# Rounding the keys to their high half on GpSimd instead of ScalarE, from the second batch on

## The chip, the cores and the metric

One core of one Trainium2 chip runs the whole program. The metric is the device time of one execution in microseconds (us). The kernel before takes 885.71 us, the median of 3 runs. PE is TensorE's matmul side and PEld its weight loads, DVE is VectorE, ACT is ScalarE, POOL is GpSimd, SP is SyncE, which here only issues DMA transfers.

## The reference

One block of a small network, in float32, on 8 batches of 512 tokens of width 256: cross-attention with 16 heads of width 16 in which the context serves as keys and as values, and then a mixture of 8 experts, of which each token uses its two best.

```python
x = x + xattn(layernorm(x), ctx, ctx, w_proj, b_proj)   # x, ctx: (8, 512, 256)
x = x + ffn(layernorm(x), Wg, W1, W2, W3)

# xattn: q = x / 2, k = cond_k / 2, 16 heads of width 16
scores = einsum('bthd,bshd->bhts', q, k)
w = softmax(scores, axis=-1)
out = einsum('bhts,bshd->bthd', w, v) @ w_proj.T + b_proj

# ffn: the top 2 of 8 experts, hidden width 682
gating = softmax(where(in_top_2, x @ Wg.T, -inf))
expert_out = (silu(x @ W1[e].T) * (x @ W2[e].T)) @ W3[e].T
out = sum over e of gating[e] * expert_out[e]
```

## The kernel before

**Precision.** A float32 operand of a matmul is split into a float16 high half and a float16 low half (the rest that the rounding leaves), and the products of the halves are summed. For the keys of batch b, `kt_in` (128 x 2 x 512, float32, 512 KB) is the loaded block, `k16[0]` its rounding to float16 and `k16[1]` the low half `kt_in - k16[0]`. There is one `kt_in`, one `k16[0]` and one `k16[1]`, used by all batches in turn. `k_stack` (two, batch b uses `b % 2`) holds for each pair of heads three bands of rows: high, low and high halves of the keys. Six DMA transfers of 128 KB each (two for each band) copy them there from `k16`: `k_part`, line 490. Queries go the same way through `x_in`, `q16`, a transpose on PE, `qt16` and `q_stack`.

**Order of the work.** There is no scheduler at run time. Each engine runs its own list of instructions strictly in order and waits on semaphores. The lists are written by one loop over slots, `for slot in range(FIRST, LAST)`, the same for every engine. A batch advances every 16 slots. A piece of work with offset `AT_...` stands in slot `16 * b + AT_...` of its engine's list. A slot is a place in a list, not a time: an engine can be ahead of another.

In each slot of the attention PE makes the scores of two units in both orientations. DVE takes the maximum of one (line 970), ACT the exponential of the other (line 839), and PE weighs the values with the exponentials (line 1294). Three pairs of PSUM banks go round between them, so that PE can be only a little ahead of DVE and ACT.

**The path of the keys.** For batch b from 1 on:
- SP, slot 16b-22: waits for `s_kl >= b` (the low half of batch b-1 is made) and loads `kt_in` of batch b (line 595). Right behind it in the same slot are the six `k_part` transfers of batch b-1, which wait for the same semaphore (line 598) and read `k16`; each adds 16 to `s_kd`.
- ACT, slot 16b-18 (`AT_K_HI`, lines 908 to 911): waits for the load (`s_kin`) and for `s_kd >= 96 b`, which says that all six transfers of batch b-1 have landed, so that `k16` is free, and rounds `kt_in` to `k16[0]`.
- POOL, slot 16b-4 (`AT_K_LO`): `low_keys`, line 691, makes `k16[1]`.

**POOL's list in the slots around.** By slot modulo 16, for the batches that are in flight at once:
- 12: `low_keys` (691), then `choose` (697 to 715), which waits for DVE's indices of the two best experts
- 14: `split_weights(e, 2)` (746 to 756), which prepares a third of an expert's weights
- 1: `pick_slots` (720 to 728)
- 2: `inverse_root` for the layer norm in front of the attention (678 to 686, `AT_X_ROOT`), `finish_rows` (733, 737) and `scatter` (eight indirect transfers, 472)
- 3: `split_weights(e, 0)`
- 4: `inverse_root` for the second layer norm (`AT_Z_ROOT`)
- 5: the low half of the queries (794, `AT_Q_LO`)
- 7: `split_weights(e, 1)`
- 8: the low half of the tokens for the experts and a copy (802, 806, `AT_Z_LO`)

`choose`, `pick_slots` and `scatter` belong to a batch whose attention is done, so they first run in the slots 44 to 50, beside the keys of batch 4. The work on ACT that needs POOL's results is `normalise` (844): on the queries in the slots 0 to 2 modulo 16 (needs `AT_X_ROOT`) and on the tokens in slot 5 (needs `AT_Z_ROOT`). ACT rounds the normalised tokens in slot 8 (928), for which POOL's line 802 waits. PE needs POOL's low half of the queries at line 1328.

After the last batch the experts run tile by tile on PE; the first tiles are interleaved with the end of the attention.

Of the kernel before, what the change touches and what calls it, by code (L numbers as in the profile page):

```python
# [99 lines left out]
AT_K_HI = -18  # L100
# [43 lines left out]
def piece_at(half_slot):  # L144
    return 0 <= half_slot - EARLY_HALF < EARLY * PIECES


def due(step, offset, of=1):

    b, left = divmod(step - offset, PER * of)  # L150
    return [b] if left == 0 and 0 <= b < B else []
# [36 lines left out]
def hold(eng, passed):  # L188

    eng.sem_inc(passed, 1)  # L190
# [53 lines left out]
def ge(eng, sem, value):  # L244
    if value > 0:
        eng.wait_ge(sem, value)
# [22 lines left out]
def build(nc, xq_l, x_l, v_l, kT_l, wp_l, bias, wg_l, w12_l, w3_l, const, out):  # L269
    ctx = ExitStack()  # L270
    with ctx:
# [3 lines left out]
        def sem(name):  # L275
            return ctx.enter_context(nc.semaphore(name))
# [84 lines left out]
        def se(name, shape, dt=F32):  # L361
            return spent.enter_context(nc.sbuf_tensor(name, shape, dt))

        x_in = se("x_in", [P, NT, W])
        kt_in = se("kt_in", [P, 2, T])
        q16 = [se(f"q16_{i}", [P, NT, W], F16) for i in range(2)]
        qt16 = [se(f"qt16_{i}", [P, 2, T], F16) for i in range(2)]
        k16 = [se(f"k16_{i}", [P, 2, T], F16) for i in range(2)]
# [38 lines left out]
        s_xin, s_kin, s_vin, s_xres_ld = sem("s_xin"), sem("s_kin"), sem("s_vin"), sem("s_xres_ld")  # L407
        s_qh, s_kh = sem("s_qh"), sem("s_kh")
        s_ql, s_kl = sem("s_ql"), sem("s_kl")
        s_qd, s_kd = sem("s_qd"), sem("s_kd")  # L410
# [258 lines left out]
        def _(pool):  # L669
# [6 lines left out]
            def inverse_root(agg, rs, sh, done, b):  # L676

                nc.gpsimd.tensor_tensor(rs[:, :], agg[:, :, 1], con[:, C_EPS:C_EPS + 1].to_broadcast([P, NT]),
                                        ALU.add).then_inc(done, 1)
                pool.wait_ge(done, b * 4 + 1)  # L680
                nc.gpsimd.tensor_tensor(rs[:, :], rs[:, :], con[:, C_POW:C_POW + 1].to_broadcast([P, NT]),
                                        ALU.pow).then_inc(done, 1)
                pool.wait_ge(done, b * 4 + 2)
                nc.gpsimd.tensor_tensor(sh[:, :], agg[:, :, 0], rs[:, :], ALU.mult).then_inc(done, 1)
                pool.wait_ge(done, b * 4 + 3)
                nc.gpsimd.tensor_tensor(sh[:, :], sh[:, :], con[:, C_NEG:C_NEG + 1].to_broadcast([P, NT]),
                                        ALU.mult).then_inc(done, 1)

            def low_keys(b):
                pool.wait_ge(s_kh, b + 1)  # L690
                nc.gpsimd.tensor_tensor(k16[1][:, :, :], kt_in[:, :, :], k16[0][:, :, :],
                                        ALU.subtract).then_inc(s_kl, 1)
# [24 lines left out]
            def pick_slots(b):  # L717

                pool.wait_ge(s_diff, b + 1)
                nc.gpsimd.tensor_tensor(ediff[:, :], con[:, C_EULER:C_EULER + 1].to_broadcast([P, NT]), diff[:, :],  # L720
                                        ALU.pow).then_inc(s_ed, 1)
                pool.wait_ge(s_ed, b + 1)
                nc.gpsimd.tensor_scalar(den[:, :], ediff[:, :], 1.0, WSCALE, ALU.add, ALU.mult).then_inc(s_den, 1)
                pool.wait_ge(s_pos, b + 1)
                if b >= 1:
                    pool.wait_ge(s_slot, b * 3)
                for c in range(2):
                    nc.gpsimd.tensor_tensor(pick[:, c, :, :], hot[:, c, :, :], pos[:, :, :],
                                            ALU.mult).then_inc(s_pick, 1)

            def finish_rows(b):

                nc.gpsimd.tensor_copy(z_row[:, :, :, W].bitcast(U32),
                                      con[:, C_TOK + b * NT:C_TOK + (b + 1) * NT].unsqueeze(1).broadcast_to([P, 2, NT])
                                      ).then_inc(s_row, 1)
                pool.wait_ge(s_gate, b + 1)
                nc.gpsimd.tensor_tensor(z_row[:, 1, :, W + 1], ediff[:, :], z_row[:, 0, :, W + 1],
                                        ALU.mult).then_inc(s_row, 1)
# [41 lines left out]
                            add_rows(k, k % 2, t, k)  # L780

            for slot in range(FIRST, LAST):
                for b in due(slot, AT_K_LO):
                    if b >= 1:
                        low_keys(b)
                for b in due(slot, AT_X_ROOT):
                    pool.wait_ge(s_prep, (b + 1) * K_STAT)
                    ge(pool, s_qn, b * NT)
                    inverse_root(mv, rstd, shift, s_rstd, b)
                    if b == 0:  # L790
                        low_keys(b)
                for b in due(slot, AT_Q_LO):
                    pool.wait_ge(s_qh, b + 1)
                    nc.gpsimd.tensor_tensor(q16[1][:, :, :], x_in[:, :, :], q16[0][:, :, :],
                                            ALU.subtract).then_inc(s_ql, 1)
                for b in due(slot, AT_Z_ROOT):
                    pool.wait_ge(s_ln2, (b + 1) * K_STAT)
                    ge(pool, s_zn, b * NT)
                    inverse_root(mv2, rstd2, shift2, s_rstd2, b)
                for b in due(slot, AT_Z_LO):  # L800
                    pool.wait_ge(s_zh, b + 1)
                    nc.gpsimd.tensor_tensor(z_row[:, 0, :, W // 2:W].bitcast(F16), z_n[:, :, :],
                                            z_row[:, 0, :, 0:W // 2].bitcast(F16), ALU.subtract).then_inc(s_zl, 1)
                    pool.wait_ge(s_zl, b + 1)
                    hold(pool, s_held[2])
                    nc.gpsimd.tensor_copy(z_row[:, 1, :, 0:W], z_row[:, 0, :, 0:W]).then_inc(s_zcp, 1)
                for b in due(slot, AT_CHOOSE):
                    choose(b)
                for b in due(slot, AT_PICK):
                    pick_slots(b)  # L810
                for b in due(slot, AT_SCATTER):
                    finish_rows(b)
                    scatter(pool, b)
                for c, off in enumerate(AT_W_LO):
                    for e in due(slot, off):
                        split_weights(e, c)
                for h in range(2):
                    add_early(2 * slot + h)
# [9 lines left out]
        def _(act):  # L828
# [65 lines left out]
            for slot in range(FIRST, LAST):  # L894
                exponentials(slot, 0)
                misc(2 * slot)
                if piece_at(2 * slot):
                    next(early)
                exponentials(slot, 1)
                for b, s in running(slot, AT_WEIGH):  # L900
                    if s % 4 == 3:
                        g = s // 4
                        q = b * 4 + g
                        act.wait_ge(s_pv, q + 1)
                        if q >= 2:
                            act.wait_ge(s_mw, misc_use((q - 2) // 4, "heads", (q - 2) % 4) + 1)
                        nc.scalar.copy(heads[q % 2][:, :], pv_bank).then_inc(s_hd, 1)  # L907
                for b in due(slot, AT_K_HI):
                    act.wait_ge(s_kin, (b + 1) * 16)
                    ge(act, s_kd, b * 96)  # L910
                    nc.scalar.copy(k16[0][:, :, :], kt_in[:, :, :]).then_inc(s_kh, 1)
                for i in range(NT):
                    for b in due(slot, AT_X_NORM[i]):
                        act.wait_ge(s_rstd, (b + 1) * 4)
                        normalise(x_in, x_in, rstd, shift, i, s_qn)
                    for b in due(slot, AT_Z_NORM[i]):
                        act.wait_ge(s_rstd2, (b + 1) * 4)
                        ge(act, s_zl, b)
                        normalise(z_n, x2, rstd2, shift2, i, s_zn)
                for b in due(slot, AT_Q_HI):  # L920
                    act.wait_ge(s_qn, (b + 1) * NT)
                    if b >= 1:
                        act.wait_ge(s_mw, misc_use(b - 1, "turn_q", 1) + 1)
                    nc.scalar.copy(q16[0][:, :, :], x_in[:, :, :]).then_inc(s_qh, 1)
                for b in due(slot, AT_Z_HI):
                    act.wait_ge(s_zn, (b + 1) * NT)
                    ge(act, s_sc, b * 128)
                    nc.scalar.copy(z_row[:, 0, :, 0:W // 2].bitcast(F16), z_n[:, :, :]).then_inc(s_zh, 1)
                misc(2 * slot + 1)
                if piece_at(2 * slot + 1):  # L930
                    next(early)
# [541 lines left out]
```

## Time and profile before

| | before |
|---|---|
| median of 3 runs | 885.71 us (885.52 to 887.39) |
| the profiled execution, its own time | 885.23 us |
| its span, first to last instruction | 883.4 us |
| mean granted TensorE clock | 0.987 of full speed |
| PE busy | 789.3 us, 89% |
| DVE busy | 602.3 us, 68% |
| ACT busy | 557.1 us, 63% |
| POOL busy | 438.9 us, 50% |

The profiled execution's own time is 1.8 us more than its span, which is what lies ahead of the first and behind the last instruction. A busy share is the mean over two stages: the attention (up to about 420 us), in which PE, DVE and ACT are all near 90%, and the experts, in which only PE is. In a timeline a row gives the start, the duration, the engine, the line and the operation; in brackets stands the time for which the engine sat idle ahead of it, and what it waited for.

### The profile page before, as it was taken

Reading aid. Unit: us, or ns where it says so; the run is one execution under the profiler, and the core shown is the slowest. Engines: PE = TensorE matmul, PEld = TensorE weight load, DVE = VectorE, ACT = ScalarE, POOL = GpSimd, SP = SyncE. Lnnn points to the kernel's source line nnn. Section 1 sums busy time; section 2 is a strip of 40 time slices with the busy share of each in tenths; the row PEclk is TensorE's granted clock in tenths of the full one; section 3 lists DMA queues with packets and bytes.
Section 4 is the critical chain, followed back from the end, with each engine's and each line's share of the span. In section 5 each row is a group of like instructions: output and inputs, shape, how many; then the busy total and the mean of one; then the engine's idle time right before and its main releaser. Section 6 shows DMA issues by size and latency. Waiting matters only on the chain.

```text
span 883.4 us, 20060 instructions
## 1 busy us (share of the span) xinstructions
PE 789.3 (89%) x6472; PEld 481.7 (55%) x6472; DVE 602.3 (68%) x1224; ACT 557.1 (63%) x970; POOL 438.9 (50%) x431
## 2 busy tenths in 40 slices
PE   0578898989989898987989999997999999999995
PEld 0112233323333333332337788886888888888884
DVE  4898888979889798899815466553555555555552
ACT  3369789788898888867784544443444444444442
POOL 4565435786767778775634574223322222222222
PEclk9999999999999999999999999998999999999998
DMA  8585656866567585674285799998996788483822
GB/s 174 170 201 167 200 128 228 181 221 153 177 234 168 203 220 178 152 173 159 87 267 175 204 267 284 287 290 223 261 254 156 174 239 256 56 251 55 246 42 24
DMA packets 105955, 167.52 MB, mean 190 GB/s; under 512 B 54688, under 2 KB 83232, under 8 KB 101280
## 3 DMA queue, kind: packets, MB, share of 16 engines
q1 hardware_dynamic: 92448, 148.76, 58.4%
q0 software_dynamic: 13440, 17.90, 10.7%
q8 instruction: 37, 0.61, 0.3%
q14 instruction: 30, 0.25, 0.1%
HBM read 119.75 MB, written 42.55 MB: 184 GB/s over the span
## 4 chain that ended last, share of the span: by engine, by line
PE 45%; DMA 2%; ACT 2%; issue 2%; SPq 1%; POOL 1%; DVE 0%; POOLq 0%; ACTq 0%; DVEq 0%
PE ps L1371 9%; PE ps L1375 9%; PE ps L1373 9%; PE ps L1389 4%; PE ps L1393 4%; PE ps L1391 4%; PE ps L1294 2%; DMA slots<-fill 1%; ACT probs L839 1%; PE ps L1279 1%; POOL slots L472 1%; PE ps L1398 1%; DMA w<-w_parts 1%; SPq L534 1%; ACT z_n L844 1%
## 5 line engine op out<-in xcount | busy, mean ns | idle before, releaser
L970 DVE TENSOR_REDUCE neg_max<-ps 128x2 f16<-128x1024 f32 x256 | 309.1, 1221 | 38.1 <-PE ps L1266 33.6
L839 ACT ACTIVATE probs<-ps 128x1024 f32<-128x1024 f32 x256 | 258.9, 1024 | 62.1 <-PE ps L1279 61.6
L766 POOL DMA_INDIRECT out<-y,aim x72 | 113.1, 1570 | 246.8 <-DVE y L1197 174.1
L1371 PE MATMUL ps<-zt,w 128*128 128x256 f16 x792 | 217.2, 274 | 6.9 <-DMA w<-w_parts 5.2
L1375 PE MATMUL ps<-zt,w 128*128 128x256 f16 x792 | 217.1, 274 | 0.0
L1373 PE MATMUL ps<-zt,w 128*128 128x256 f16 x792 | 217.1, 274 | 0.0
L873 ACT ACTIVATE silu<-ps 128x256 f32<-128x256 f32 x216 | 82.5, 382 | 190.6 <-PE ps L1375 188.3
L1178 DVE SCALAR_TENSOR_TENSOR hid<-ps,silu 128x256 f32<-128x256 f32 x216 | 91.6, 425 | 133.9 <-ACT silu L873 130.5
L1294 PE MATMUL ps<-probs,v_ext 128*32 128x512 f32 x1024 | 139.8, 618 | 5.3 <-ACT heads L907 4.4
L1266 PE MATMUL ps<-k_stack,q_stack 48*128 48x512 f16 x512 | 104.4, 407 | 34.5 <-ACT probs L839 17.7
L1279 PE MATMUL ps<-q_stack,k_stack 49*128 49x512 f16 x512 | 102.3, 397 | 7.2 <-DVE neg_max L970 7.0
L1389 PE MATMUL ps<-w,hid 128*128 128x256 f16 x360 | 98.1, 273 | 0.0
L1393 PE MATMUL ps<-w,hid 128*128 128x256 f16 x360 | 98.1, 273 | 0.0
L1391 PE MATMUL ps<-w,hid 128*128 128x256 f16 x360 | 98.1, 273 | 0.0
L1371 PEld LDWEIGHTS ps<-zt,w 128*128 128x128 f16 x792 | 77.9, 98 | 22.3 <-issue 12.2
L1279 PEld LDWEIGHTS ps<-q_stack,k_stack 49*128 49x128 f16 x512 | 24.7, 93 | 113.8 <-issue 78.8
L1373 PEld LDWEIGHTS ps<-zt,w 128*128 128x128 f16 x792 | 77.9, 98 | 9.4
L1375 PEld LDWEIGHTS ps<-zt,w 128*128 128x128 f16 x792 | 77.9, 98 | 9.4
L881 ACT CAST hid<-hid 128x256 f16<-128x256 f32 x180 | 72.0, 400 | 8.4 <-DVE hid L1178 5.4
L1185 DVE TENSOR_TENSOR hid<-hid 128x256 f16<-128x256 f32 x180 | 76.2, 423 | 1.5
L472 POOL DMA_INDIRECT slots<-z_row,slot_u x64 | 63.1, 985 | 24.4 <-issue 19.9
L756 POOL TENSOR_TENSOR w_lo<-w_in,w_hi 128x1408 f16<-128x1408 f32 (+1 forms) x24 | 70.6, 2944 | 2.0
(126 smaller groups left out, 907.5 us busy)
## 6 DMA issues: line engine op xcount, KB each, us to landing
w<-w_parts SPq DMA_DIRECT2D x36, 1408.0 KB
w<-w_parts SPq DMA_DIRECT2D x36, 768.0 KB
w_in<-in_w SPq DMA_DIRECT2D x16, 704.0 KB, 5.2
v_ext<-in_v SPq DMA_DIRECT2D x8, 1024.0 KB, 5.5
k_stack<-k SPq DMA_DIRECT2D x48, 128.0 KB, 5.0
q_stack<-qt SPq DMA_DIRECT2D x48, 128.0 KB, 4.6
w_in<-in_w SPq DMA_DIRECT2D x8, 768.0 KB, 5.1
w_parts<-w_hi SPq DMA_DIRECT2D x16, 352.0 KB, 2.3
```

The costliest lines, as they stand in the source:

```text
L766: nc.gpsimd.indirect_dma_start(out=out, out_offset=bass.IndirectOffsetOnAxis(ap=aim[frm][:, t, 0:1].bitcast(U32), axis=0), in_=y[frm][:, t ...
L839: nc.scalar.activation(probs[g % 2][:, j:j + 2, k, :], pair_banks[PLACE["exp", u] % 3], ACT.Exp, scale=0.25).then_inc(s_exp, 1)
L970: nc.vector.tensor_reduce(neg_max[b % 2][:, i, c:c + 3:2], pair_banks[PLACE["max", u] % 3], AX.X, ALU.max, negate=True).then_inc(s_red, 1)
L1266: mm = nc.tensor.matmul(to[:, par, :], q_stack[r][rows, a, i * P:(i + 1) * P], k_stack[r][rows, a, :], start=True, stop=True)
L1279: mm = nc.tensor.matmul(to[:, par, :], k_stack[r][rows, a, k * P:(k + 1) * P], q_stack[r][rows, a, :], start=True, stop=True)
L1294: mm = nc.tensor.matmul(pv_bank[32 * n:32 * n + 32, :], v_ext[b % 2][:, j, 4 * g + n, :], probs[g % 2][:, n, j, :], start=(j == 0), stop=( ...
L1371: nc.tensor.matmul(dst, w[:, kk, 1, cols], z16[:, kk, :], start=(kk == 0), stop=False)
L1373: nc.tensor.matmul(dst, w[:, kk, 0, cols], z16[:, 2 + kk, :], start=False, stop=False)
L1375: mm = nc.tensor.matmul(dst, w[:, kk, 0, cols], z16[:, kk, :], start=False, stop=(kk == 1))
L1389: nc.tensor.matmul(y_bank[t], h[1], w3[par][:, 0, m, :], start=first, stop=False, skip_group_check=True)
L1391: nc.tensor.matmul(y_bank[t], h[0], w3[par][:, 1, m, :], start=False, stop=False, skip_group_check=True)
L1393: nc.tensor.matmul(y_bank[t], h[0], w3[par][:, 0, m, :], start=False, stop=False, skip_group_check=True)
```

## The change

From batch 1 on, the rounding of the keys stands in POOL's list instead of ACT's, in the same slot 16b-18, with the same two waits and one for the rounding of the batch before. It is the first thing in its slot there: behind `low_keys` of batch b-1 and `choose`, ahead of `split_weights(e, 2)`. ACT keeps the rounding of batch 0. SP's list and all transfers stay as they are.

```diff
             for slot in range(FIRST, LAST):
+                for b in due(slot, AT_K_HI):
+                    if b >= 1:
+                        pool.wait_ge(s_kin, (b + 1) * 16)
+                        pool.wait_ge(s_kd, b * 96)
+                        pool.wait_ge(s_kh, b)
+                        nc.gpsimd.tensor_copy(k16[0][:, :, :], kt_in[:, :, :]).then_inc(s_kh, 1)
                 for b in due(slot, AT_K_LO):
                     if b >= 1:
                         low_keys(b)
...
                 for b in due(slot, AT_K_HI):
-                    act.wait_ge(s_kin, (b + 1) * 16)
-                    ge(act, s_kd, b * 96)
-                    nc.scalar.copy(k16[0][:, :, :], kt_in[:, :, :]).then_inc(s_kh, 1)
+                    if b == 0:
+                        act.wait_ge(s_kin, 16)
+                        nc.scalar.copy(k16[0][:, :, :], kt_in[:, :, :]).then_inc(s_kh, 1)
```

## Rows read from the trace of the kernel before

**Rows 1.** Waits from 150 to 400 us: total us, times, longest us.

```profile
POOL z_row L802 <- ACT z_row L928: 17.7, 5, 4.3
...
POOL pick L728 <- DVE pos L1039: 5.7, 5, 1.1
...
PE ps L1328 <- POOL q L794: 4.2, 4, 1.3
...
ACT z_n L844 <- POOL shift L686: 1.1, 4, 0.5
```

**Rows 2.** Groups of instructions by line: busy us, mean ns, idle before.

```profile
L911 ACT CAST k<-kt_in 128x1024 f16<-128x1024 f32 x8 | 8.3, 1039 | 9.2 <-DMA kt_in<-in_k_t 9.2
...
L749 POOL CAST w_hi<-w_in 128x1408 f16<-128x1408 f32 (+1 forms) x24 | 33.4, 1392 | 1.6
...
L806 POOL COPY z_row<-z_row 128x1024 f32<-128x1024 f32 x8 | 8.3, 1037 | 1.4 <-POOL z_row L802 1.4
```

**Rows 3.** Timeline of POOL beside the keys of batch 4.

```profile
153.74 2.12 POOL L691 TENSOR_TENSOR k<-kt_in,k 128x1024 f16<-128x1024 f32 x1
...
160.28 1.47 POOL L746 TENSOR_SCALAR w_in<-w_in 128x1536 f32<-128x1536 f32 x1
...
169.58 0.46 POOL L728 TENSOR_TENSOR pick<-hot,pos 128x32 f32<-128x32 f32 x2 [1.13 <-DVE pos L1039]
...
171.65 0.20 POOL L686 TENSOR_TENSOR shift<-shift,con 128x4 f32<-128x4 f32 x1
...
190.81 2.13 POOL L794 TENSOR_TENSOR q<-x_in,q 128x1024 f16<-128x1024 f32 x1
```

**Rows 4.** Timeline of SP: the six transfers of the keys of batches 1 and 3.

```profile
52.04 3.95 SPq L490 DMA_DIRECT2D k_stack<-k  x6
...
156.33 3.94 SPq L490 DMA_DIRECT2D k_stack<-k  x6
```

**Rows 5.** From issue to landing: load of batch 4, last key transfer of batches 3 to 6, 1.

```profile
DMA to landing us min/median/max: 4.5/4.5/4.5
...
DMA to landing us min/median/max: 6.1/6.1/6.1
...
DMA to landing us min/median/max: 5.6/5.6/5.6
...
DMA to landing us min/median/max: 5.8/5.8/5.8
...
DMA to landing us min/median/max: 4.9/4.9/4.9
...
DMA to landing us min/median/max: 7.3/7.3/7.3
```

**Rows 6.** Timeline of ACT: its first steps that need POOL, in three batches.

```profile
72.36 0.59 ACT L844 ACTIVATE x_in<-x_in,shift,rstd 128x256 f32<-128x256 f32 x1
...
173.72 0.59 ACT L844 ACTIVATE x_in<-x_in,shift,rstd 128x256 f32<-128x256 f32 x1
...
190.89 2.07 ACT L844 ACTIVATE z_n<-x,shift,rstd 128x256 f32<-128x256 f32 x4 [0.51 <-POOL shift L686]
...
203.24 1.03 ACT L928 CAST z_row<-z_n 128x1024 f16<-128x1024 f32 x1
...
244.55 2.08 ACT L844 ACTIVATE z_n<-x,shift,rstd 128x256 f32<-128x256 f32 x4 [0.22 <-POOL shift L686]
...
255.47 1.03 ACT L928 CAST z_row<-z_n 128x1024 f16<-128x1024 f32 x1
```

**Rows 7.** Busy time by stretch (PE, PEld, DVE, ACT, POOL), then granted clock.

```profile
196.00:198.00 2.00, 2.00 (x12) 0.20 (x8) 1.23 (x1) 1.16 (x2) 1.85 (x3) 0.50 0.97 401
...
302.00:304.00 2.00, 2.00 (x12) 0.20 (x8) 1.23 (x1) 1.10 (x2) 1.92 (x2) 0.50 0.94 393
```

**Rows 8.** Timeline of POOL beside the keys of batch 2.

```profile
56.10 1.47 POOL L746 TENSOR_SCALAR w_in<-w_in 128x1536 f32<-128x1536 f32 x1 [6.48 <-DMA w_in<-in_w]
...
62.93 0.20 POOL L678 TENSOR_TENSOR rstd<-mv,con 128x4 f32<-128x4 f32 x1
```

## The prediction

> **What bounds the kernel now.** I read the busy shares first, and they lead astray here: in the attention PE, DVE and ACT are all about nine tenths busy, and POOL less, so taking work from ACT looks right. A share says nothing about which wait ends last, so I went on to the waits of the stretch from 150 to 400 us, where the steady state of the attention lies [rows 1]. In all four batches there whose queries are still prepared, ACT waits for POOL's `shift` ahead of the second layer norm (1.1 us in four waits), and PE waits for POOL's low half of the queries (4.2 us in four waits). The waits are short, but they say that the least busy engine arrives last at these two places. POOL in turn waits for ACT's high half of the tokens, 17.7 us in five waits. That is a ring, and I followed it through the timelines. POOL's `shift`, the last step of `inverse_root`, releases ACT's layer norm at 190.89, and at 203.24 ACT starts the rounding of the tokens, which takes 1.03 [rows 6]; then POOL's lines 802, 806 and `low_keys`, `choose`, `split_weights`, `pick_slots`, `scatter`, `split_weights` follow one another up to the next `inverse_root`, 53.7 us after the last one by ACT's two starts of 190.89 and 244.55. A microsecond more on POOL between line 802 and line 686 is a microsecond more per batch, unless a wait on POOL's own part of the ring takes it up. ACT's rounding of the keys stands in slot 14 modulo 16, outside ACT's part of the ring (slots 5 to 8).
>
> **What leaves ACT.** Seven roundings of 1.04 us each, 7.3 us [rows 2]. From batch 4 on I count nothing for them, since ACT then waits for POOL anyway. For batches 1 to 3 the ring has not closed (`choose` to `scatter` are not running yet); bounds there are a gain of 3 x 1.04 = 3.1 us and, if POOL's delay reaches ACT, a loss of the same.
>
> **What the copy costs on POOL.** The trace has no such copy there. The nearest rows are a float32 copy of the same shape, 1037 ns, and a rounding to float16 of a larger block, 1392 ns [rows 2]; these are the bounds, and I take 1.04, as the larger block scaled to 1024 elements gives 1.01. The Trainium skill ("GPSIMD Engine Reference", section "Performance versus the Vector engine") speaks against moving elementwise work here: about 2.6 cycles for an element at 1.2 GHz. By that the copy would take an estimated 2.2 us, and the four copies that count below would cost 4.7 us more; the same page sets operations with one input apart, and the rows above bear that out, so the sum goes by the rows.
>
> **What the wait costs on POOL.** This is the main term. On ACT the two waits had long been met when ACT got there. POOL gets there much earlier, because `low_keys` of the batch before, whose end starts both the load and the six transfers that free `k16`, is POOL's own last work but `choose`. For batch 4:
> - `low_keys` ends at 153.74 + 2.12 = 155.86 [rows 3]. SP's six transfers begin at 156.33 and take 3.94 to issue [rows 4], so the last begins at 156.33 + 3.94 x 5/6 = 159.6. It lands 6.1 later [rows 5], at 165.7. The load of `kt_in` is issued just ahead of the six and lands 4.5 after its issue [rows 5], by 160.8, so it isn't the last.
> - In the list before, `split_weights` starts at 160.28 [rows 3], right behind `choose`. With the copy in front it starts at 165.7 + 1.04 = 166.75: 6.5 late.
>
> `low_keys`, the issue and `split_weights` keep these distances within 0.1 us for batches 5, 6 and 7; only the landing of the last transfer differs: 5.6, 5.8 and 4.9 in place of 6.1 [rows 5]. So the delay is the landing plus 0.37: 6.5, 6.0, 6.2 and 5.3, together 23.9 us.
>
> What takes it up: `pick_slots` waited 1.13 for DVE's prefix sums [rows 3], in every batch [rows 1]. These come at PE's pace and don't hang on the delayed work of the same batch, so that wait goes: 4 x 1.13 = 4.5. Behind it nothing on POOL waits up to the second `inverse_root` and the queries' low half (190.81), whose weights had been loaded in time. Left: 23.9 - 4.5 = 19.4 us.
>
> Where the stall goes: first to DVE, which needs POOL's gate denominators for the slots of the tokens, and to ACT, which in the old timing starts the queries' layer norm at 173.72 [rows 6], 1.9 after POOL's `shift` at 171.85 [rows 3]; that becomes 171.85 + 5.4 = 177.2, so ACT stands for over 4 us, and through the PSUM banks PE and DVE do too. These are the same microseconds, not further ones. The transfers themselves are unchanged; SP, which waits for `split_weights` to store the weights, is late by the same.
>
> **The clock.** In two of the four batches PE's wait for the queries is followed by a fall of the clock (0.50 granted, 1.2 of 2.4 GHz [rows 7]). In the first of these, ACT's part of the ring took 203.24 - 190.89 = 12.35; in a batch without it, 255.47 - 244.55 = 10.92 [rows 6]. Longer stalls should bring it to the other two batches: 0 to 2 x 1.43 = 2.9 us; I take half, 1.4.
>
> **The early batches.** For batch 2, the last of six transfers begins at 52.04 + 3.95 x 5/6 = 55.3 [rows 4] and lands 7.3 later [rows 5], at 62.6; the copy ends at 63.7; `split_weights`, which ran from 56.10 to 62.93 [rows 8], ends at 70.5, and `inverse_root` about 1.9 later, at 72.4. ACT's first use was at 72.36 [rows 6]. So the delay, 7.6 us, just fits, and eats what ACT saved by its missing rounding. The same holds for batch 3 as far as I see. I take 0 for the three.
>
> Sum: 19.4 + 1.4 + 0 = 20.8 us over the profiled execution's 885.23: 906.0. The median of the runs shown is 0.5 above that execution, which gives 906.5.
>
> **Rivals.**
> - *ACT decides* (faster). If POOL had some 6 us to spare at the two `inverse_root`s, ACT's 7 x 1.04 = 7.3 us would come off: 878.4. For it: ACT is near nine tenths busy. Against: POOL is the one waited for at these places in four batches of four [rows 1]. 0.06.
> - *No net change*. If the transfers landed by the time POOL gets there, each copy would cost 1.04 and take away a wait of 1.13: 885.7. It needs landings 5.4 us earlier than any row shows. 0.07.
> - *POOL wins part back*. POOL waits 17.7 / 5 = 3.5 us per batch for ACT's tokens [rows 1]. If ACT, with 1.04 less to do, were there earlier, up to 4 x 3.5 = 14.2 of the 20.8 would come back: 892 to 900. Against: ACT can't start this part before POOL's `inverse_root`. 0.10.
> - *The stalls spread*. Each late batch gets two stalls, at the queries' and at the tokens' layer norm; if each drops the clock in the open, that is 8 falls in place of 2, 6 x 1.43 = 8.6, and batches 2 and 3 overrun by up to 1.04 each: 885.7 + 19.4 + 8.6 + 2.1 = 916. 0.12.
> - The forecast: 0.65, by its own terms from 885.7 + 19.4 - 3.1 = 902 to 885.7 + 23.9 + 2.9 + 1.0 = 913.5.
>
> **Numbers.** Slower by over 0.2% (1.8 us, about what a measurement of this kernel can tell from no change): 0.65 + 0.10 + 0.12 = 0.87; within it 0.07; faster 0.06. For the range I leave out the two cases at or below 886 (0.13) and the far end of the fourth rival: 895 to 914, which takes in most of the third.
>
> **What the changed profile would show.** Seven copies on POOL of about 1.04 us. Ahead of the later four, an idle time of about 5 us that a transfer of the keys ends. `split_weights` right behind. No wait for DVE's prefix sums at line 728. DVE waiting for POOL at line 1022 and ACT for POOL's `shift` at line 844, in the queries' norm too, where it didn't wait in the steady state. ACT's second layer norms about 58 to 59 us apart in the late batches, not 53.7. The experts' stage as long as before. I would be wrong if POOL's idle time ahead of the copy were short, or if it were long and line 844 still didn't wait.

## The result, and the profile after

The change makes the kernel slower. Its median is 906.5 us (903.25 to 909.2, 4 runs) against 885.62 us (881.93 to 887.39, 4 runs): a ratio of 1.0249, with a 95% interval of 1.0217 to 1.0281. (The ratios in this document are those on record, taken over the runs; the quotient of the two medians would be 1.0236.) The medians lie 20.9 us apart; 20.8 were forecast. The profiled execution after takes 908.37 us, its span is 906.6 us and its mean granted clock 0.968. It lies 1.9 above its median, where the one before lay 0.4 below its own, so the two traces stand 23.2 us of span apart.

In the kernel after, the line numbers from `normalise` on are higher by 6 (844 is now 850, 802 is 808, 1022 is 1028), and the new copy is line 788.

The busy times show the edit, ACT 5.5 us less than before and POOL 7.7 us more, and PE 13.1 us more at a lower mean clock. They don't show where the time is lost.

```profile
PE 802.4 (89%) x6472; PEld 484.7 (53%) x6472; DVE 603.3 (67%) x1224; ACT 551.6 (61%) x963; POOL 446.6 (49%) x438
```

The waits from 150 to 420 us tell more: total us, times, longest us. ("issue" means that the profile shows no semaphore event which ended the wait.)

```profile
POOL k L788 <- issue: 20.3, 4, 5.6
POOL z_row L808 <- ACT z_row L934: 19.0, 5, 5.7
...
DVE z_row L1028 <- POOL den L723: 14.3, 4, 4.0
...
ACT x_in L850 <- POOL shift L686: 12.0, 4, 3.5
...
PE ps L1314 <- DVE x L1067: 11.7, 4, 3.4
POOL top_f L697 <- DVE top_e L1021: 10.4, 5, 2.1
...
PE ps L1334 <- POOL q L800: 3.9, 4, 1.0
```

In the kernel before, four of these lines don't exist in the same stretch: POOL ahead of the copy, DVE for POOL's gate denominators, ACT for POOL's `shift` ahead of the queries' layer norm, and PE for DVE. Of POOL's five waits for the prefix sums at line 728 (5.7 us) one is left, of 1.1 us. This is one stall seen at four places: POOL stands some 5 us in each of four batches, DVE and ACT stand because POOL is late, and PE stands because DVE is.

What ends POOL's wait is seen by putting two timelines side by side, SP's and POOL's, beside the keys of batch 4, with the time from issue to landing of the last of SP's six transfers (begun at 161.5). First SP:

```profile
157.74 0.34 SPq L595 DMA_DIRECT2D kt_in<-in_k_t  x1
158.18 3.90 SPq L490 DMA_DIRECT2D k_stack<-k  x6
...
DMA to landing us min/median/max: 5.9/5.9/5.9
```

Then POOL:

```profile
155.58 2.13 POOL L691 TENSOR_TENSOR k<-kt_in,k 128x1024 f16<-128x1024 f32 x1
...
167.51 1.04 POOL L788 CAST k<-kt_in 128x1024 f16<-128x1024 f32 x1 [5.35 <-issue]
168.53 1.47 POOL L746 TENSOR_SCALAR w_in<-w_in 128x1536 f32<-128x1536 f32 x1
...
176.64 0.46 POOL L728 TENSOR_TENSOR pick<-hot,pos 128x32 f32<-128x32 f32 x2
...
178.71 0.20 POOL L686 TENSOR_TENSOR shift<-shift,con 128x4 f32<-128x4 f32 x1
...
196.37 0.20 POOL L678 TENSOR_TENSOR rstd<-mv,con 128x4 f32<-128x4 f32 x1 [0.29 <-DVE mv L988]
...
224.46 1.04 POOL L788 CAST k<-kt_in 128x1024 f16<-128x1024 f32 x1 [4.26 <-issue]
...
283.01 1.04 POOL L788 CAST k<-kt_in 128x1024 f16<-128x1024 f32 x1 [5.57 <-issue]
...
341.09 1.04 POOL L788 CAST k<-kt_in 128x1024 f16<-128x1024 f32 x1 [5.16 <-issue]
```

The last transfer lands at 161.5 + 5.9 = 167.4, and the copy starts at 167.51. No instruction stands between, and the other wait of the copy was over: the load, begun at 157.74, landed 4.1 later, at 161.8. The other three batches agree: their last key transfers land at 219.5 + 4.8 = 224.3, 276.7 + 6.2 = 282.9 and 335.3 + 5.7 = 341.0, just ahead of the copies at 224.46, 283.01 and 341.09. The delay of a batch is this idle time and the copy itself: 6.4, 5.3, 6.6 and 6.2, together 24.5 us. From `low_keys` of batch 3 (153.74 before, [rows 3]; 155.58 after), which stands just ahead of the first late copy, to that of batch 7 (365.73 before, 387.41 after) the distance grows by 231.83 - 211.99 = 19.8 us. Of the rest of the 23.2, 1.8 us lie ahead of it: 0.4 where ACT waits for POOL's `shift` in batch 3, and some 1.5 at a fall of the granted clock (0.50 from 144 to 146) that the kernel before doesn't have there. 1.5 us lie behind it.

ACT's timeline shows who waits at the queries' norm:

```profile
178.95 0.60 ACT L850 ACTIVATE x_in<-x_in,shift,rstd 128x256 f32<-128x256 f32 x1 [3.28 <-POOL shift L686]
...
198.28 2.08 ACT L850 ACTIVATE z_n<-x,shift,rstd 128x256 f32<-128x256 f32 x4 [0.21 <-POOL shift L686]
209.20 1.03 ACT L934 CAST z_row<-z_n 128x1024 f16<-128x1024 f32 x1
255.52 2.08 ACT L850 ACTIVATE z_n<-x,shift,rstd 128x256 f32<-128x256 f32 x4 [0.22 <-POOL shift L686]
```

ACT's stretch from `z_n` to line 934 now takes 209.20 - 198.28 = 10.92, the value that the kernel before had without a fall of the clock [rows 6]. The fall hasn't gone, it has moved. By stretches of 2 us (PE, PEld, DVE, ACT, POOL, granted clock, DMA share, GB/s):

```profile
176.00:178.00 2.00, 0.00 (x0) 0.00 (x0) 1.01 (x6) 0.00 (x0) 1.83 (x6) 0.75 0.89 349
178.00:180.00 2.00, 1.45 (x8) 0.43 (x8) 2.00 (x2) 1.05 (x3) 1.06 (x5) 0.50 1.00 323
180.00:182.00 2.00, 2.00 (x11) 0.24 (x10) 1.44 (x2) 0.93 (x2) 1.49 (x2) 0.50 0.21 87
182.00:184.00 2.00, 2.00 (x11) 1.22 (x9) 0.00 (x0) 0.00 (x0) 1.69 (x2) 0.54 0.37 133
184.00:186.00 2.00, 1.31 (x13) 0.41 (x16) 1.76 (x3) 1.62 (x3) 1.39 (x2) 1.00 0.27 99
```

PE does nothing from 176 to 178, and the granted clock is 0.50 (1.2 of 2.4 GHz) from about 177 on, for some 7 us. What PE waits for is DVE:

```profile
178.00 0.58 PE L1314 MATMUL ps<-ident,neg_max 128*4 128x128 f16 x4 [3.18 <-DVE x L1067]
```

All four late batches show such a fall, at 176, 234, 292 and 350. But little of the fall shows: POOL, late as it is, scatters and splits weights meanwhile, and DVE's statistics of the second layer norm come 0.29, 0.84, 0.79 and 0.80 after POOL gets there, 2.7 us in all. In the kernel before POOL doesn't wait for them in these batches.

### The profile page after: what moved, and what is told of

Its sections match the earlier page's. It is cut to its first block, busy times and chain, and to the rows that moved or that the text cites. A ratio compares the mean times of both kernels' runs of the same rounds, so it can differ in the third digit from the quotient of the medians.

```text
span 906.6 us, 20060 instructions
## 1 busy us (share of the span) xinstructions
PE 802.4 (89%) x6472; PEld 484.7 (53%) x6472; DVE 603.3 (67%) x1224; ACT 551.6 (61%) x963; POOL 446.6 (49%) x438
## 3 DMA queue, kind: packets, MB, share of 16 engines
q0 software_dynamic: 13440, 17.90, 10.4%
## 4 chain that ended last, share of the span: by engine, by line
PE 46%; ACT 3%; issue 2%; DVE 2%; DMA 2%; SPq 1%; POOL 1%; POOLq 0%; ACTq 0%; DVEq 0%
PE ps L1377 9%; PE ps L1379 9%; PE ps L1381 9%; PE ps L1395 4%; PE ps L1397 4%; PE ps L1399 4%; PE ps L1300 3%; ACT probs L845 1%; PE ps L1285 1%; DVE neg_max L976 1%; DMA slots<-fill 1%; PE ps L1272 1%; POOL slots L472 1%; PE ps L1404 1%; PE ps L1328 1%
## 5 line engine op out<-in xcount | busy, mean ns | idle before, releaser
L1300 PE MATMUL ps<-probs,v_ext 128*32 128x512 f32 x1024 | 144.1, 636 | 5.4 <-ACT heads L913 4.5
L1272 PE MATMUL ps<-k_stack,q_stack 48*128 48x512 f16 x512 | 106.7, 416 | 31.2 <-ACT probs L845 14.4
L1285 PE MATMUL ps<-q_stack,k_stack 49*128 49x512 f16 x512 | 104.6, 406 | 7.9 <-DVE neg_max L976 7.8
```

Of the source, the lines that this page charges most:

```text
L1272: mm = nc.tensor.matmul(to[:, par, :], q_stack[r][rows, a, i * P:(i + 1) * P], k_stack[r][rows, a, :], start=True, stop=True)
L1285: mm = nc.tensor.matmul(to[:, par, :], k_stack[r][rows, a, k * P:(k + 1) * P], q_stack[r][rows, a, :], start=True, stop=True)
L1300: mm = nc.tensor.matmul(pv_bank[32 * n:32 * n + 32, :], v_ext[b % 2][:, j, 4 * g + n, :], probs[g % 2][:, n, j, :], start=(j == 0), stop=( ...
```

## The experiments

Two theories were set against each other. **The wait:** POOL arrives at the moved wait about 5 us before the last key transfer lands, and this stands on the path through POOL. **The work:** the copy takes POOL's time and moves a bound; where it stands matters little. Each ratio is against the kernel before, run on the same chip; its medians there are 884.14 us (experiments 1 to 4), 884.23 (5 to 8), 882.89 (9 to 11) and 882.74 (12).

**1. The waits alone (on the kernel before).** ACT still rounds.

```diff
+                for b in due(slot, AT_K_HI):
+                    if b >= 1:
+                        pool.wait_ge(s_kin, (b + 1) * 16)
+                        pool.wait_ge(s_kd, b * 96)
                 for b in due(slot, AT_K_LO):
```

> ScalarE keeps the rounding; GpSimd only gets the two waits (load landed, six key transfers landed) in its slot 16b-18. Theory (the wait is the cost): GpSimd stands 4.3 to 5.6 us ahead of split_weights in the late four batches, 20.3 us in the trace of the changed kernel, less the 4 x 1.13 us that pick_slots no longer waits: 885.6 + 15.8 = 901 us, 897 to 905. Rival (the copy itself on GpSimd is the cost, by its time or by contention): no more than 888 us.

Measured: 902.34 us, ratio 1.0209 (1.0173 to 1.0245). The waits of this kernel, from 150 to 400 us:

```profile
POOL w_in L746 <- issue: 20.8, 4, 5.7
...
DVE z_row L1026 <- POOL den L723: 10.7, 4, 3.2
...
ACT x_in L848 <- POOL shift L686: 8.3, 4, 2.5
```

The wait without the copy costs 902.34 - 884.14 = 18.2 us. The new waits for POOL are here too; only the first line has another name, since `split_weights` is now the instruction behind the wait. In this trace the distance from `low_keys` of batch 3 to that of batch 7 is 15.5 us longer than in the kernel before (153.03 to 380.53); with the whole change it was 19.8. The 4.3 between them are about the four copies of 1.04. The medians can't tell as much: against the kernel before on its own chip the whole change costs 20.9 and the waits 18.2, and the runs of either kernel lie up to 6 us apart.

**2. The copy alone (on the kernel before).** A copy of 1.04 us into an unused tile at the same place, for batches 4 to 7, with a wait that has long been met.

```diff
...
+                for b in due(slot, AT_K_HI):
+                    if b >= 4:
+                        pool.wait_ge(s_zcp, b - 3)
+                        nc.gpsimd.tensor_copy(spare[:, :, :], z_row[:, 1, :, 0:W])
                 for b in due(slot, AT_K_LO):
```

> ScalarE keeps the rounding; GpSimd makes, in slots 16b-18 of batches 4 to 7, an additional copy of the same size and types from a block that has long been there into a spare one, with nothing to wait for. It does no useful work. Theory: 4 x 1.04 us more on GpSimd against 4 x 1.13 us that pick_slots waited anyway: 885.6 us, 884 to 888, and the wait at pick_slots falls from 1.13 to about 0.1 us. Rival (the copy is the cost): 895 us and more.

Measured: 884.44 us, ratio 1.0016 (0.9996 to 1.0035). POOL's wait for the prefix sums takes it up, as the prediction said: of the first such wait, 1.13 us in [rows 3], this is left, and the other three are as short.

```profile
168.17 0.46 POOL L729 TENSOR_TENSOR pick<-hot,pos 128x32 f32<-128x32 f32 x2 [0.15 <-DVE pos L1044]
```

**3. The whole change with two high halves.** The rounding of batch b goes to a buffer of its own parity, so that it needs the transfers of batch b-2, long landed. `low_keys` takes over the wait for those of batch b-1.

```diff
+        k_high = [k16[0], se("k16_2", [P, 2, T], F16)]
...
-                        pool.wait_ge(s_kd, b * 96)
+                        ge(pool, s_kd, (b - 1) * 96)
                         pool.wait_ge(s_kh, b)
-                        nc.gpsimd.tensor_copy(k16[0][:, :, :], kt_in[:, :, :]).then_inc(s_kh, 1)
+                        nc.gpsimd.tensor_copy(k_high[b % 2][:, :, :], kt_in[:, :, :]).then_inc(s_kh, 1)
...
                 pool.wait_ge(s_kh, b + 1)
+                ge(pool, s_kd, b * 96)
...
```

> The changed kernel with a second buffer for the high half, used in turn, so that GpSimd's rounding waits for the key transfers of two batches before and not of the last one; the load stays to be waited for. Theory: the load lands about 0.1 us after GpSimd gets there, so the wait falls from 5 us to under 1 us and the copy of 1.04 us hides in the wait of pick_slots: 886 us, 884 to 889. Rival (GpSimd is the wrong engine for it wherever it waits): stays at 900 us or above.

Measured: 886.0 us, ratio 1.0019 (1.0000 to 1.0038). In the window from 150 to 400 us one wait ahead of the copy is left, of 0.16 us, and a name stands beside it now: the load of `kt_in`.

```profile
213.79 1.04 POOL L791 CAST k<-kt_in 128x1024 f16<-128x1024 f32 x1 [0.16 <-DMA kt_in<-in_k_t]
```

The four waits ahead of the copy are what the change cost: without them and with all copies in place the time is that of the kernel before within 0.4%, so that 3.4 us at most are left for the copies.

**4. The same rounding later in POOL's list**, at 16b-8, ahead of the low half of the tokens, with its waits unchanged.

```diff
-                for b in due(slot, AT_K_HI):
+                for b in due(slot, -8):
                     if b >= 1:
                         pool.wait_ge(s_kin, (b + 1) * 16)
```

> The changed kernel with the rounding ten slots later in GpSimd's list (16b-8 in place of 16b-18), ahead of line 802, where GpSimd stood idle 2.6 to 4.3 us for ScalarE's tokens in the late batches, and where load and transfers have long landed. Theory: the copy hides in that idle time, no wait is left: 885.6 us or up to 3.1 us less for what ScalarE saves in the first batches, 882 to 887. Rival (GpSimd's copy costs its time wherever it stands): 4 to 7 x 1.04 us more, 890 to 893 us.

Measured: 884.29 us, ratio 0.9996 (0.9976 to 1.0016). The timeline of POOL:

```profile
200.59 1.03 POOL L788 CAST k<-kt_in 128x1024 f16<-128x1024 f32 x1
...
203.15 2.13 POOL L808 TENSOR_TENSOR z_row<-z_n,z_row 128x1024 f16<-128x1024 f32 x1 [1.53 <-ACT z_row L934]
```

The transfers have landed and POOL would have waited for ACT here anyway, so the copy costs nothing. The test says more: ACT is relieved of seven roundings, 7.3 us, and this brings nothing either; by the interval at most 0.24%, 2.1 us.

**5 and 6. What a microsecond on POOL costs at two places (on the kernel before).** Two copies of 1.04 us into unused tiles for four batches: in one kernel behind `scatter`, in the other ahead of POOL's wait for ACT's tokens.

```diff
...
                     scatter(pool, b)
+                    if b <= 3:
+                        for extra in spare:
+                            nc.gpsimd.tensor_copy(extra[:, :, :], z_row[:, 1, :, 0:W])
```

```diff
...
                 for b in due(slot, AT_Z_LO):
+                    if 1 <= b <= 4:
+                        pool.wait_ge(s_zcp, b)
+                        for extra in spare:
+                            nc.gpsimd.tensor_copy(extra[:, :, :], z_row[:, 1, :, 0:W])
                     pool.wait_ge(s_zh, b + 1)
```

Behind `scatter`:

> The kernel before, and on GpSimd, right behind the scatter of the batches 0 to 3, two more copies of 1.04 us that do no useful work and wait for nothing. They stand on GpSimd's part of the ring (line 802 to line 686), behind the wait of pick_slots. Theory (each microsecond there is a microsecond per batch): 4 x 2 x 1.02 = 8.2 us over the 884.1 us of the kernel before, 892 us, 889 to 895. Rival (GpSimd has time to spare and only the long wait overran it): 884 to 886 us.

Ahead of the wait for the tokens:

> The same two copies as in ring_on, but ahead of line 802 of the batches 1 to 4, where GpSimd stood idle 2.6 to 4.3 us for ScalarE's tokens. Theory: hidden, 884.1 us, 882 to 886. Rival (more work on GpSimd costs its time wherever it stands): 892 us.

Measured: behind `scatter` 899.0 us, ratio 1.0150 (1.0114 to 1.0186); ahead of the wait 884.32 us, ratio 1.0008 (0.9985 to 1.0032). The place decides, as expected, but the first lies above the 889 to 895 expected: it costs 14.8 us where the copies take 4 x 2.07 = 8.3. ACT's timeline of that kernel shows where the rest is:

```profile
195.17 2.07 ACT L848 ACTIVATE z_n<-x,shift,rstd 128x256 f32<-128x256 f32 x4 [2.44 <-POOL shift L687]
208.21 1.03 ACT L932 CAST z_row<-z_n 128x1024 f16<-128x1024 f32 x1
251.45 2.08 ACT L848 ACTIVATE z_n<-x,shift,rstd 128x256 f32<-128x256 f32 x4 [2.16 <-POOL shift L687]
264.35 1.03 ACT L932 CAST z_row<-z_n 128x1024 f16<-128x1024 f32 x1
```

The windows of the same kernel:

```profile
198.00:200.00 2.00, 1.72 (x8) 0.82 (x6) 1.14 (x1) 1.98 (x3) 1.05 (x1) 0.51 0.97 344
200.00:202.00 2.00, 2.00 (x14) 0.33 (x12) 0.86 (x2) 1.57 (x2) 1.85 (x3) 0.50 1.02 414
```

From `z_n` to the rounding of the tokens ACT takes 208.21 - 195.17 = 13.04 and 264.35 - 251.45 = 12.90, where a batch without a fall takes 10.92 (13.09 and 12.93 in the two batches behind these). The longer wait for `shift` is followed by a fall of the clock in all four batches, and here nothing covers it, for POOL itself waits for ACT's tokens at the end of this stretch. So a batch pays about 2.0 for the copies and 2.1 for the clock: 251.45 - 195.17 = 56.28 us, against 52.22 for a batch of the kernel before without a fall (244.55 to 296.77); the next two take 56.14 and 56.34. Over four batches that is 4 x 4.06 = 16.2, less the two short falls that the kernel before has by itself (2.9): 13.3 of the 14.8 measured.

**7. The change's rounding behind `scatter`**, 16b-14: a real rounding of 1.04 us on the path, its waits long met.

```diff
...
                     scatter(pool, b)
+                for b in due(slot, -14):
+                    if b >= 1:
+                        pool.wait_ge(s_kin, (b + 1) * 16)
+                        pool.wait_ge(s_kd, b * 96)
+                        pool.wait_ge(s_kh, b)
+                        nc.gpsimd.tensor_copy(k16[0][:, :, :], kt_in[:, :, :]).then_inc(s_kh, 1)
```

> The changed kernel with the rounding four slots later on GpSimd (16b-14, behind the scatter). The key transfers have long landed there, so no wait is left, but the copy stands on the ring. Theory: 4 x 1.04 = 4.2 us over the kernel before, 888 us, 886.5 to 890, against the same copy in slot 16b-8, which cost nothing. Rival (only the wait ever cost anything): 884 us.

Measured: 891.83 us, ratio 1.0095 (1.0059 to 1.0132): 7.6 us. The direction is as expected, the size again above the copies' own 4.2 and the 890 expected at most. ACT's part of the ring:

```profile
243.08 2.08 ACT L850 ACTIVATE z_n<-x,shift,rstd 128x256 f32<-128x256 f32 x4 [1.18 <-POOL shift L686]
256.09 1.03 ACT L934 CAST z_row<-z_n 128x1024 f16<-128x1024 f32 x1
...
353.76 2.08 ACT L850 ACTIVATE z_n<-x,shift,rstd 128x256 f32<-128x256 f32 x4 [1.17 <-POOL shift L686]
364.69 1.03 ACT L934 CAST z_row<-z_n 128x1024 f16<-128x1024 f32 x1
```

It takes 13.01 in the first of these batches, so the fall is here too, and 13.15 in the next. In the batch before them, with a wait of 0.61 us for `shift`, it took 10.92; in the last one it took 10.93 although the wait, 1.17, is the same. So the wait alone doesn't decide whether the clock falls. This trace is of the fastest run, 887.95 us, only 3.7 above the kernel before; that more such falls make the rest of the median's 7.6 is argued, not shown.

**8. Time taken from POOL ahead of `choose`** (on the kernel of experiment 4, here kernel 4). ACT makes the copy of line 806 in a later slot, so that POOL saves 1.04 us per batch.

```diff
-                    pool.wait_ge(s_zl, b + 1)
-                    hold(pool, s_held[2])
-                    nc.gpsimd.tensor_copy(z_row[:, 1, :, 0:W], z_row[:, 0, :, 0:W]).then_inc(s_zcp, 1)
...
+                for b in due(slot, 46):
+                    act.wait_ge(s_zl, b + 1)
+                    nc.scalar.copy(z_row[:, 1, :, 0:W], z_row[:, 0, :, 0:W]).then_inc(s_zcp, 1)
```

> The kernel with the rounding on GpSimd in slot 16b-8, and in return ScalarE makes GpSimd's copy of the tokens' rows (line 806) in slot 14 modulo 16, where its own rounding of the keys stood. GpSimd's part of the ring is 1.2 us shorter. Theory: VectorE's statistics for the second layer norm came only 0.4 us ahead of GpSimd, so they take over as what GpSimd waits for: 4 x 0.4 = 1.6 us less, 882.5 us, 881 to 884. Rival (nothing else is near the bound): 4 x 1.2 = 4.8 us less, 879 us. Another (ScalarE is itself at the bound in that slot): no gain, 884 to 888 us.

Measured: 886.13 us, ratio 1.0010 (0.9991 to 1.0029), no gain: the 881 to 884 expected are missed. The time is that of the last rival, but the reason named there, ACT, isn't what the trace shows. The waits from 150 to 400 us say where the microsecond went:

```profile
POOL top_f L697 <- DVE top_e L1021: 16.4, 5, 3.3
...
POOL pick L728 <- DVE pos L1045: 5.6, 5, 1.1
```

POOL arrives earlier at `choose` and waits there for DVE's indices, 16.4 us in place of the 10.4 of the kernel before and of kernel 4; at line 728 nothing has changed.

**9 to 11. An attempt to gain.** PE waits 4.2 us for the queries' low half [rows 1], so this was moved up in POOL's list, with a third of the weights behind it (its store in SP's list four slots later) and `low_keys` six slots earlier; once on the kernel before, once with the rounding on POOL right ahead of `low_keys` (at 16b-11), once with the rounding in the slot of the change.

```diff
-AT_K_LO = -4
+AT_K_LO = -10
...
-AT_Q_LO = -11
+AT_Q_LO = -13
...
-AT_W_LO = (3, 7, 14)
-AT_W_OUT = (1, 9, 13)
+AT_W_LO = (4, 7, 14)
+AT_W_OUT = (5, 9, 13)
```

With the rounding on ACT:

> The kernel before (rounding on ScalarE) with GpSimd's list in another order: the low half of the queries ahead of the second inverse_root, the first split_weights behind it, and low_keys right after, in GpSimd's idle time, ten slots ahead of its old place; SyncE stores the first third of the weights four slots later. Theory (the bound is GpSimd's stretch from pick_slots to the queries' low half, tied with the other engines): TensorE's wait for the queries of 1.0 to 1.3 us and the clock falls behind it go away, the batches shrink to 51 to 52 us from 52.2 to 53.7: 877 to 882 us. Rival (the rest is tied with it so closely that nothing comes): 883 to 886 us.

With the rounding on POOL, ahead of `low_keys`:

> The same order, and the rounding on GpSimd, one slot ahead of low_keys, in the same idle time, with nothing left to wait for. If ScalarE is the next bound once GpSimd no longer is, its 1.04 us less per batch shows: 2 to 6 us below reorder_act. If TensorE or VectorE is, the two come out the same within 1.5 us.

With the rounding on POOL, in the slot of the change:

> The same order with the rounding where the change put it (16b-18, ahead of split_weights(e, 2)). As low_keys now runs early, SyncE starts load and key transfers when its own list gets there and no longer right when GpSimd ends low_keys. Theory (the wait is the distance from that start to GpSimd's arrival): the transfers start some 4 to 5 us earlier against GpSimd's arrival, the wait falls from 5 us to 0 to 2 us, and the time is at most 8 us above reorder_pool. Rival (the slot itself is bad): 20 us above it, as the change did.

Measured: 913.38 (ratio 1.0350, 1.0323 to 1.0378), 907.81 (1.0278, 1.0241 to 1.0314) and 936.71 us (1.0588, 1.0552 to 1.0623), beside 882.89 of the kernel before. All three are far slower than the kernel before, where 877 to 882 were expected of the first. The second lies 5.6 below the first, within the 2 to 6 that were to show ACT as the next bound, but it doesn't show that: the waits of the first, from 40 to 420 us, have another reason for it.

```profile
POOL q L794 <- ACT q L924: 53.9, 6, 19.2
...
ACT k L911 <- DMA k_stack<-k: 16.1, 6, 6.5
```

ACT, at its old place, now stands for the key transfers itself, 16.1 us, since they start late; in the second kernel the rounding waits for nothing. The other line is the price of moving the queries' low half up: POOL now waits there for ACT's rounding of the queries, 53.9, 54.9 and 31.8 us in the three kernels against 3.9 in the kernel before.

In the second, SP's list shows why the transfers start late. They stand behind the store of a third of the weights. That was so in the kernel before too, but there the store was out (203.66) before `low_keys` released the transfers; here `low_keys` ends at 216.50, and the store waits for POOL's `split_weights` until 224.63.

```profile
224.65 0.34 SPq L509 DMA_DIRECT2D w_parts<-w_hi  x1
...
226.79 4.24 SPq L490 DMA_DIRECT2D k_stack<-k  x6
232.47 3.83 SPq L495 DMA_DIRECT2D q_stack<-qt  x6
```

The last transfer of the queries, begun at 235.7, lands 7.0 later, at 242.7, and PE's first scores of the batch start right behind that, after a wait:

```profile
242.78 0.39 PE L1272 MATMUL ps<-k_stack,q_stack 48*128 48x512 f16 x2 [2.32 <-issue]
```

How much of the time each of these waits costs was not tested. The third, in which the transfers start late and the rounding stands early, makes the moved wait longer: 63.1 us in six waits from 40 to 420 us, where the kernel of the change has 49.9. First the kernel of the change, then the third:

```profile
POOL k L788 <- issue: 49.9, 6, 18.0
...
POOL k L788 <- issue: 63.1, 6, 14.9
```

In the late four batches that is 34.2 in place of 20.3. So the expectation is missed, at its root: the wait was to shrink to 0 to 2 us, and the third kernel to lie at most 8 us above the second; it lies 28.9 above. The rival (the slot itself) named 20. That the wait and the time grow together while the copy keeps its size fits the first theory, but several things moved at once here, and this doesn't prove it.

**12. `scatter` later** (on the kernel before): `scatter` and `finish_rows` three slots later, behind a third of the weights and the queries' low half.

```diff
-AT_Q_LO = -11
+AT_Q_LO = -13
-AT_W_LO = (3, 7, 14)
+AT_W_LO = (2, 7, 14)
...
-                for b in due(slot, AT_SCATTER):
-                    finish_rows(b)
-                    scatter(pool, b)
+                for late in range(2):
+                    for b in due(slot, AT_SCATTER + 3 * late):
+                        if late == (b < 5):
+                            finish_rows(b)
+                            scatter(pool, b)
```

> The kernel before, rounding on ScalarE, with GpSimd's scatter of the batches 0 to 4 (10.2 us) three slots later, behind the second inverse_root, and the queries' low half and the first split_weights ahead of it: the stretch from pick_slots to the queries' low half is some 10 us shorter, and SyncE's list is left as it was. Theory (that stretch is the bound, tied with the other engines): TensorE no longer waits 1.0 to 1.3 us for the queries, the clock falls behind that wait go, 3 to 6 us less: 878 to 881 us. Rival (the scatter lands too late for ScalarE's line 928, which overwrites its rows): no gain, 884 us and more.

Measured: 900.12 us, ratio 1.0214 (1.0180 to 1.0248), and not the gain expected. PE's wait for the queries is gone, and a wait of ACT has come, the one that the rival named: its rounding of the tokens writes the buffer that `scatter` reads.

```profile
257.89 1.04 ACT L930 CAST z_row<-z_n 128x1024 f16<-128x1024 f32 x1 [1.62 <-DMA slots<-z_row,slot_u]
```

These waits add up to 4.4 us in four. POOL waits for ACT's rounding of the queries here too, 19.3 us in four from 150 to 400. The rest of the 17.4 was not traced to its place and stays open.

## Why the prediction was right, step by step

- **The copy.** 1.04 us on POOL was forecast, 1.04 measured. The doubt that the Trainium skill ("GPSIMD Engine Reference", section "Performance versus the Vector engine") raised, an estimated 2.2 us by its rate per element, isn't borne out by this row; the rows of [rows 2] were the better guide.
- **The wait.** The delays were to be 6.5, 6.0, 6.2 and 5.3, together 23.9; they were 6.4, 5.3, 6.6 and 6.2, together 24.5. The landings vary from batch to batch: the second delay was 0.7 shorter than forecast and the last 0.9 longer. That the sum held within 0.6 is partly luck. Experiment 1 shows the wait without the copy, experiments 2 and 3 the copy without the wait.
- **What takes it up.** 4 x 1.13 = 4.5 us of waits at line 728 went, as experiment 2 shows. Left: 24.5 - 4.5 = 20.0, and the four batches are 19.8 longer.
- **Where it shows.** DVE at line 1028 and ACT at the queries' norm, both new. ACT's second layer norms stand 57.2, 58.5 and 58.1 us apart; 58 to 59 were forecast.
- **The early batches** cost nearly nothing, and for the reason given: POOL's two waits there are the longest of all, 11.5 and 18.0 us, but it had idle time. ACT's first use of the queries' norm moved from 72.36 to 72.56 in batch 2. In batch 3, which the forecast took over without a sum, POOL came later than the idle time allowed, and ACT waited 0.42 us (121.52 became 122.24).
- **The clock: the mis-sized term.** +1.4 was expected, as the short falls at the tokens' norm would come in all four batches. They came in none: ACT's part of the ring took 10.92 in each, and so the price of 2 x 1.43 = 2.9 in the kernel before was saved. In their place came the long falls ahead, at the queries' norm, and 2.7 us of POOL's wait for DVE behind them. The net is about -0.2, and 20.0 - 0.2 = 19.8 is what the four batches grew by. The sum wasn't hurt, since the term was small.
- **The ring: right for one part, too simple for another.** The prediction held that a microsecond on POOL anywhere from line 802 to line 686 is one per batch, unless a wait on POOL's own part takes it up. Behind `pick_slots` it costs that, and in most batches a fall of the clock besides (experiments 5 and 7). Of the waits on POOL's own part it counted the one at line 728 and left out the one at `choose`, 10.4 us in five. From line 802 to `choose` taking time away gains nothing (experiment 8); that up to about 2 us more would cost nothing there follows from that wait, but was not tested. What binds POOL starts at `pick_slots`, where it waits for DVE's prefix sums.
- **The sum: luck in the last digit.** The two profiled executions lie 908.37 - 885.23 = 23.1 us apart, of which the forecast's terms make 19.8; the 1.8 ahead and the 1.5 behind the four batches were not in it. That the medians of four runs each lie 20.9 apart, 0.1 from the forecast, is luck: the runs after span 903.25 to 909.2.

Of the rivals, *ACT decides* and *POOL wins part back* fell with experiment 4, where ACT's 7.3 us bring nothing; and POOL's wait for ACT's tokens, of which the second would have used up a part, is as long as before (19.0 and 17.7 us). *No net change* is what the edit does when its waits are met (experiments 3 and 4). *The stalls spread* was right that every late batch has a fall; but it had two in each, and there was one, and its price was wrong: 2.7 us in all, as read above, in place of 8.6 more.

## What to carry to other kernels

When an instruction moves to another in-order engine, look first at when each engine gets to its waits. Here the same waits had long been met on the one and took 5 us per batch on the other, which arrived just behind the work that starts the transfers; the 1 us of work alone, at that place, cost nothing that could be measured (experiment 2). The same instruction was free where its new engine idled anyway and the transfers had landed (experiment 4), and a second buffer freed it at the place of the change (experiment 3); on the path behind `scatter` it cost 7.6 us with its waits met (experiment 7). The attempts to gain repeat the lesson: the instructions moved up met waits that had not been seen at their old places. Relieving ACT by 7.3 us (experiment 4) or POOL by 4 x 1.04 (experiment 8) gained nothing measurable here.

## What the runs showed of the hardware that was not expected

- A batch of the attention lasts 52.2 us, or 53.7 when the granted clock falls to 0.50 behind PE's wait for the queries [rows 7]. Nearly the same wait is followed by a fall in some batches and by none in others: of PE's waits of 1.26, 0.97, 0.97 and 0.96 us the first and third were. That this makes the spread of the runs (881.0 to 887.9 over 29 runs of the kernel before on one chip) is argued from the traces, not shown.
- In the kernel after, PE's wait of 2.1 to 3.4 us for DVE went with a fall in all four batches, and behind some 7 us of half clock POOL waited only 0.3 to 0.8 us for DVE, being late itself. With ACT's wait for `shift` at 2 us and nothing to cover the fall, it cost about 2.1 us each (experiment 5). The Trainium skill ("TensorE: Matmul & The Clock Gate", section "HAM oscillation — how this bites in real kernels") tells of bursts that each start at the low clock behind a wait; the trace agrees as to the fall, and what it costs depends on who is late at the time.
